# Decoder kernel: the transpose and the row of the softmax maxima move from behind step 0 to behind step 1 of the next unit's maximum pass

## The reference

```python
att = jnp.einsum('bhqd,bhkd->bhqk', q, k) * scale
causal = jnp.tril(jnp.ones((T, T), bool))
att = jnp.where(causal[None, None], att, -jnp.inf)
y = jnp.einsum('bhqk,bhkd->bhqd', jax.nn.softmax(att, axis=-1), v)
...
attc = jnp.einsum('bhqd,bhkd->bhqk', qc, kc) * scale
y = y + jnp.einsum('bhqk,bhkd->bhqd', jax.nn.softmax(attc, axis=-1), vc)
y = y.transpose(0, 2, 1, 3).reshape(x.shape[0], T, C)
return y @ Wp + bp
```

## Time and profile before

| | |
|---|---|
| median of 3 runs | 750.29 us (749.99 to 752.45) |
| the profiled execution | 749.41 us, its span in the trace 747.6 us |
| PE busy | 619.9 us (83%) |
| DVE busy | 536.1 us (72%) |
| ACT busy | 427.3 us (57%) |
| POOL busy | 221.6 us (30%) |
| attention block, both passes | about 74 to 400 us of the span |
| transposes (line 692) | 16, the first at 80.0, the last at 363.3 us |

### The profile page before, as it was taken

One profiled execution on the slowest core, in us unless ns is written; L12 is line 12 of the kernel. 1 busy time (PEld: TensorE's weight loads), 2 busy tenths in 40 slices (PEclk: granted clock), 3 DMA queues, 4 the chain that ended last, 5 costly groups with the idle time before them and its releaser, 6 DMA issues. The chain is left out here.

```text
span 747.6 us, 13476 instructions
## 1 busy us (share of the span) xinstructions
PE 619.9 (83%) x5150; PEld 340.1 (45%) x5150; DVE 536.1 (72%) x701; ACT 427.3 (57%) x769; POOL 221.6 (30%) x259
## 2 busy tenths in 40 slices
PE   7978899999999999999896399997106698969996
PEld 5645333333333333333332277873002366637884
DVE  5378889999999999999352567992886557756442
ACT  3555578888888888888961244556431122244224
POOL 7227522344444655555200020000520380005000
PEclk9999989999999999999997589999657779998999
DMA  8348576556555544442002195420000400000000
GB/s 194 117 120 260 196 215 148 141 132 150 145 140 142 137 89 90 109 85 61 17 1 64 39 393 172 160 78 0 0 0 0 156 0 1 1 1 0 1 0 29
DMA packets 41084, 70.76 MB, mean 95 GB/s; under 512 B 11332, under 2 KB 30108, under 8 KB 40512
## 3 DMA queue, kind: packets, MB, share of 16 engines
q1 hardware_dynamic: 30128, 33.98, 18.0%
q0 software_dynamic: 10288, 33.71, 14.0%
q10 hardware_dynamic: 608, 2.25, 1.4%
HBM read 44.84 MB, written 24.79 MB: 93 GB/s over the span
## 5 line engine op out<-in xcount | busy, mean ns | idle before, releaser
L908 ACT ACTIVATE prob<-ps 128x512 f32<-128x512 f32 (+2 forms) x480 | 253.4, 582 | 48.7 <-PE ps L703 40.9
L1027 DVE TENSOR_REDUCE pm<-ps 128x2 f32<-128x1024 f32 x192 | 226.0, 1216 | 7.7 <-PE ps L665 5.9
L726 PE MATMUL ps<-prob,vst 128*9 128x256 f32 (+1 forms) x1664 | 130.1, 385 | 10.1 <-ACT o_all L896 10.1
L703 PE MATMUL ps<-qq,kc 50*128 50x256 bf16 (+1 forms) x832 | 133.6, 275 | 0.1
L665 PE MATMUL ps<-kc,qq 48*128 48x512 bf16 x384 | 116.3, 388 | 5.6 <-DVE pm L1027 4.6
L703 PEld LDWEIGHTS ps<-qq,kc 50*128 50x128 bf16 (+1 forms) x832 | 52.0, 96 | 93.7 <-ACT prob L908 69.9
L1816 ACT ACTIVATE prob<-s 128x512 f32<-128x512 f32 (+1 forms) x28 | 15.9, 567 | 57.5 <-PE s L1748 57.5
L726 PEld LDWEIGHTS ps<-prob,vst 128*9 128x9 f32 (+1 forms) x1664 | 25.1, 88 | 51.7 <-ACT prob L908 39.1
L1034 DVE TENSOR_REDUCE nm<-ps 128x4 f32<-128x512 f32 (+1 forms) x32 | 30.7, 958 | 15.3 <-PE ps L653 15.3
L665 PEld LDWEIGHTS ps<-kc,qq 48*128 48x128 bf16 x384 | 33.0, 93 | 15.9 <-DVE pm L1027 11.1
L653 PE MATMUL ps<-masks_b 64*128 64x256 bf16 x256 | 37.4, 269 | 0.0
(11 more groups left out here) (348 smaller groups left out, 1325.5 us busy)
## 6 DMA issues: line engine op xcount, KB each, us to landing
kc<-kc_scr SPq DMA_DIRECT2D x32, 300.2 KB, 5.2
comb_bc<-comb_scr SPq DMA_DIRECT2D x8, 512.0 KB, 4.6
kc_scr<-hi POOLq DMA_DIRECT2D x9, 400.2 KB, 4.4
below<-rden_scr POOLq DMA_DIRECT2D x13, 256.0 KB, 9.6
ctx<-ctx_scr POOLq DMA_DIRECT2D x1, 3204.0 KB, 16.3
raw<-in_wexp POOLq DMA_DIRECT2D x8, 384.0 KB, 3.3
exp_scr<-raw_high POOLq DMA_DIRECT2D x8, 384.0 KB, 3.8
exp_scr<-raw_low POOLq DMA_DIRECT2D x8, 384.0 KB, 6.2
```

What stands on the lines that cost most here:

```text
L703: last = pe.matmul(bank[0:p, j * TQ:(j + 1) * TQ], kc[s][rows, j, t * 128:t * 128 + p], qq[s][rows, 0, j, :], start=(j == 0), stop=True, s ...
L726: last = pe.matmul(o_ps[32 * hh:32 * hh + VW, kind * TQ + q0:(kind + 1) * TQ], value[:, hh * VW:(hh + 1) * VW], prob[0:k, (NST * n + t) % ...
L908: act.activation(prob[0:p, g % P_RING, 2 * e:2 * e + 2, q0:TQ], s2[0:p, k % S2_RING, 0:2 * w].rearrange("p (i q) -> p i q", i=2), ACT.Exp, ...
L1027: dve.tensor_reduce(pm[:, m % 2, c, :, jt], banks, AX.X, ALU.max).then_inc(s1_read, 1)
```

## The change

A constant TURN_BEHIND says behind which maximum step of unit m the transpose of unit m - 1 and DVE's two row instructions stand. It is 1; before, the place was fixed behind step 0. The order list, PE's two loops and DVE's loop follow it. Nothing is added or taken away; the last unit's transpose and row stay where they were, so 15 of 16 transposes move.

```diff
-HALVES, TURN = 15, -1
+HALVES, TURN, TURN_BEHIND = 15, -1, 1
...
             for m in range(NU):
-                s1_order.append((m, 0))
+                s1_order += [(m, i) for i in range(TURN_BEHIND + 1)]
                 if m:
                     s1_order.append((m - 1, TURN))
-                s1_order += [(m, i) for i in range(1, HALVES)]
+                s1_order += [(m, i) for i in range(TURN_BEHIND + 1, HALVES)]
...
                         score_part(m, i, 0).then_inc(s1_ready, 1)
-                        if i == 0 and m:
+                        if i == TURN_BEHIND and m:
                             turn_maxima(m - 1)
...
                         scores_t(n, t, 1, 1)
-                        if more and i == 0:
+                        if more and i == TURN_BEHIND:
                             turn_maxima(m - 1)
...
                             reduce_half(m, i)
-                            if m and i == 0:
+                            if m and i == TURN_BEHIND:
                                 row(m - 1)
```

## The result

The changed kernel takes 766.51 us, the median of 4 runs (763.3 to 769.38), beside 751.03 us (749.99 to 752.45) for the kernel before on the same chip. The ratio is 1.0171, 95% interval 1.0125 to 1.0216: slower by 1.7%, outside the predicted range of 749.3 to 755.6. A ratio is formed from the executions of both kernels; it is not the quotient of the two medians, which would be 1.0206 here. In the experiments, an execution over 1.5% longer than the fastest of its kernel is left out of the median and of the ratio. The profiled execution took 764.99 us, its span is 763.2 us.

What follows compares the result with a forecast made beforehand. The prediction held that no engine is full and a loop of waits at the unit boundary sets the pace; 0.6 + 0.2 + 0.8 = +1.6 us took the profiled 749.41 to 751.0, median 751.9, range 749.3 to 755.6.

Steps and rivals of the forecast that it cites:

- What bounds the kernel: At the unit boundary: no engine is full; a loop of waits among PE, DVE and the ring sets the 18.68 us unit.
- The steady boundary, +0.03 to +0.05 each: At 14 unit boundaries: one PE turn (1.09) in the loop is exchanged for one reduction (1.14), +0.6 us taken in all.
- Steps 1 to 3: At the boundary: (m, 1) comes 1.1 us earlier; the turn after the transpose 0.31 earlier; (m, 2) waits 0.35, 0.05 later.
- The first moved transpose, +0.2: In the part without exponents: 0.58 us of row work moves behind (m, 1), some comes back; bounds 0 and +0.58.
- the rival with the low clock: PE's half-clock stretch at 90 to 98 us goes: 749.9 us, or 749.1 with no late row; chance 0.06.
- The transfers of the row, +0.8 with an upper bound of 5.5: SP's four row copies start 1.1 us later in 14 units; one late unit's wait, or two halves, was taken.
- the slower rival: Row copies late in three to five units: +2.9 to +6.3 us, 753.2 to 756.6; chance 0.32.
- The rule of the Trainium skill: Row copies: DMA engines take turns between queues, so a small copy stands behind other queues' packets; speaks against the change.
- fixed cost of about 2 us: Row copies: by this figure per transfer none would be late and the transfers' term would be 0; the prediction didn't follow it.
- SP's loads at no cost: Loads behind the row copies in SP's queue start 1.1 us later; the unit's other work hides them, no cost taken.
- The rival of 0.31: At the boundary: PE's free rhythm starts 0.31 us earlier, 14 times, 4.3 off, 746.0; chance 0.03.

Runs made afterwards that it cites:

- The shared form: Kernel before, with transpose in free columns of step 1's tile, steps reordered, broadcast waiting for the row: 741.06 us; four loads in place of the wait: 751.16.
- Groups 3 to 5: Changed kernel, broadcast waiting for the row: 752.82 us (kernel before: 751.51); without broadcast: 752.38. Kernel before, only SP's copies later: 766.77; with that wait too: 752.91.
- the repeated run: The changed kernel again with no edit: 765.69 us, ratio 1.015.
- group 6: Kernel before, with the expert's writes waiting for the first half of the row tile: 752.11 us; with the broadcast waiting for the whole tile: 756.46.
- group 7: Changed kernel with an early POOL load cut in two: 766.15 us; with the broadcast as four loads: 760.11; kernel before with the four loads: 751.9.
- a lead of 6: Kernel before with the maximum pass ahead by 6 turns in place of 7 (S1_LEAD): 764.48 us, ratio 1.0126.
- the spread broadcast: Changed kernel with POOL's broadcast as four loads of 32 rows each, no wait added: 760.11 us, ratio 1.0086.

## Why the prediction was wrong

- **What bounds the kernel** held: ring, reduction and PE's turns set the unit. The shared form shows it from the other side, since a turn taken out of the ring, with the new order of the steps, is worth 0.96 us in each unit.
- **The steady boundary, +0.03 to +0.05 each**, held: quiet distances went from 18.67 to 18.71. Steps 1 to 3 are in the rows: L692 waits 0.50 for pm, ACT is dry for 1.16, PE's free rhythm starts 3.78 behind the start of reduction 14 (268.75 - 264.97) where it started 3.75 behind it (253.41 - 249.66). PE's weight load of L665 waits for pm up to 0.3, where it was 0.2, as was said.
- **The first moved transpose, +0.2**, can't be told from the runs. The profiled first unit is 0.7 shorter, with a half clock of about 3.4 us in it where before it was about 6.8, so something of the rival with the low clock came here by chance; in the other traces of the moved transpose it is -0.4 to +0.5 against the 21.85 of before. The prediction also left out that row 0's copies, which move as well, would be waited for (2.1 us).
- **The transfers of the row, +0.8 with an upper bound of 5.5**, is the step that failed. That copies come late and PE waits was right and also stood as the slower rival; how late, behind what, and at what price was not. It rested on "If they land as late after their issue again, PE waits 0.7 to 1.1 there". They didn't: the copies of row 4 landed 9.3 behind their issue where it had been under 6.45. Moved by 1.14, the last two were issued behind the broadcast, where only the last had been, and by 0.14. Groups 3 to 5 show that the landings of 9 us need the broadcast; the order of issue isn't the whole of it, since row 7 of the repeated run had the same order and landed in 4.4. The measured term is 5.35 + 5.9 for two rows, and about 0.7 for the distances behind them, so 12 us in place of 0.8.
- Within that step three readings were at fault. It named POOL's expert and context writes and left out the third transfer in the same queue, the broadcast; taking that one out of the way gives back all (752.82). It judged the new place by the GB/s of stretches, but row 4's was the less loaded of the two, 245 against 270, so this figure didn't tell a late row. And it priced a late row by its lateness alone, while PE's stand of 3.90 brought a half-clock stretch that made it 5.36.
- The rule of the Trainium skill, page "DMA: Bandwidth & Descriptors" (section "Queues, rings and completion order"), of turns between queues, cited against the change, has the right sign: the traces agree for rows 4 and 6, with 9.30 us in place of 6.45 in row 4. The Trainium skill's fixed cost of about 2 us (same page, section "Anatomy of one DMA") would have made the term 0, and the traces are against that.
- **SP's loads at no cost** held: no wait for kc or ks is in PE's list. The rival of 0.31 didn't come; the distance would have had to fall below 18.6.
- The rest of the measured difference, 3.9 in the profiled pair, lies ahead of all moved instructions, with half-clock stretches near 50 and 70 us that vary between executions of one program.

What stays open: why rows 4 and 6 are caught and odd rows are not, even row 7 of the repeated run with the broadcast at +0.83. An expectation of group 6 says that broadcasts at +0.80 to +0.85, with both writes ahead, went with 9.3 us; that row, already measured then, had both writes ahead too and is against it. The number of the engine on which a packet ran isn't in the trace, and the one try to shift it (group 7) left the late rows where they were.

## What to carry to other kernels

When an edit moves a small transfer that something waits for, list what each queue issues in the 2 us around its new place; a large transfer that comes ahead of more of it can cost several times the shift (5.4 and 5.9 us a row here for a shift of 1.1). A wait on the big transfer, which had slack, was worth 14 us here for one line. And where a loop hangs on a ring of buffers, taking a turn out of the ring pays (0.96 us for each unit, and only as long as no row is late: 741.06 with the wait, 751.16 without), while moving it only exchanges one wait for another.

## What the runs showed of the hardware

- Four copies of 2 KB, issued within 2.1 us, landed 3.8 us behind the first issue in quiet units. With the broadcast 0.8 behind the first copy, rows 4 and 6 landed in 9.3 us, and row 7 of the repeated run in 4.4. With the broadcast made to wait for them they landed in 3.7 to 5.8 us in the loop.
- A broadcast of 256 KB from 4 rows to 128 partitions landed in 8.4 us, in four loads of 64 KB each in 3.2. A plain write of 384 KB landed in 2.7 to 4.1, and in 4.0 to 6.1 in the kernel whose broadcast waits for the row (medians).
- PE stood for 3.90 and 3.97 us, and each time the granted clock fell to 0.50 while it stood and stayed there for about 6.8 us, in which matmuls of L665 took 0.60 in place of 0.39. In the kernel before with a lead of 6 a stand of 2.42 us left the clock at 1.00 and cost 21.16 - 18.67 = 2.49:

```profile
296.69 0.28 PE L703 MATMUL ps<-qq,kc 50*128 50x256 bf16 x1 [2.42 <-DMA qq<-mrow]
```

```profile
297.00:301.00 4.00, 3.32 (x47) 1.25 (x43) 3.65 (x4) 3.64 (x7) 0.71 (x1) 1.00 0.07 18
```

  But with the spread broadcast a stand of 2.21 us was followed by a half-clock stretch of 3.4, and without the broadcast one of 1.39 us as well, so the length of the stand alone doesn't decide.
- The same instructions in front of the first combination took from 79.6 to 83.6 us, with half-clock stretches near 50 us in some executions and not in others.
